# Attention over a convolution block: which PSUM banks hold the turned maxima, the sums and the fourth projection tile, and when the reciprocals run

## What is computed

```
K, Q, V = conv1x1(X, Wq, bq), conv1x1(X, Wk, bk), conv1x1(X, Wv, bv)   # 8 heads of 64
M   = einsum('bhmn,bhen->bhme', K, V)          # 64 x 64 per head
Out = conv1x1(einsum('bhme,bhmn->bhen', M, Q), Wo, bo) + X
x1  = batch_norm(Out)                          # over batch and points

xn      = group_norm(x1)                       # 32 groups
q, k, v = split(w_qkv @ xn + b_qkv)            # 8 heads of 64
weight  = softmax(q.T @ k / sqrt(64))          # 1024 x 1024 per head
out     = x1 + w_proj @ (v @ weight.T) + b_proj
```

## Time and profile before

| | us |
|---|---|
| median of 3 runs | 2682.73 (2681.97 to 2682.75) |
| the profiled execution | 2683.36 |
| its span, first to last instruction | 2681.8 |
| PE busy | 2582.5 (96%) |
| DVE busy | 1621.5 (60%) |
| POOL busy | 1164.3 (43%) |
| ACT busy | 964.6 (36%) |
| mean granted clock of PE | 0.99 of full |

### The profile page before, as it was taken

One profiled execution on the slowest core, in us unless ns is written; L12 is line 12 of the kernel. 1 busy time (PEld: TensorE's weight loads), 2 busy tenths in 40 slices (PEclk: granted clock), 3 DMA queues, 4 the chain that ended last, 5 costly groups with the idle time before them and its releaser, 6 DMA issues.

```text
span 2681.8 us, 38121 instructions
## 1 busy us (share of the span) xinstructions
PE 2582.5 (96%) x13876; PEld 1710.9 (64%) x13876; DVE 1621.5 (60%) x1756; ACT 964.6 (36%) x1154; POOL 1164.3 (43%) x590
## 2 busy tenths in 40 slices
PE   7999999997999999999999999999999999999998
PEld 6888888886655665565557555755665565557554
DVE  6555455545576737755764667467647746664665
ACT  3333223332343433433442443343433433432433
POOL 4230000000276546564573676375654645761762
PEclk9999999999999999999999999999999999999999
DMA  5330111113202230231205111401231141103001
GB/s 185 130 132 33 47 47 63 63 63 111 110 24 79 87 126 24 95 128 70 102 17 181 40 79 61 152 24 80 102 110 41 78 175 38 79 18 109 17 16 63
DMA packets 64195, 214.34 MB, mean 80 GB/s; under 512 B 9152, under 2 KB 9152, under 8 KB 63168
## 3 DMA queue, kind: packets, MB, share of 16 engines
q1 hardware_dynamic: 49504, 159.41, 16.5%
q0 software_dynamic: 14560, 52.96, 5.4%
HBM read 141.05 MB, written 71.30 MB: 79 GB/s over the span
## 4 chain that ended last, share of the span: by engine, by line
PE 72%; DVE 15%; issue 6%; POOL 4%; ACT 2%; DVEq 0%; ACTq 0%; POOLq 0%
PE psum L1135 16%; PE psum L1380 14%; PE psum L1363 11%; PE psum L1320 7%; PE psum L1154 6%; PE psum L1330 5%; DVE a_all L999 4%; POOL a_all L528 4%; PE psum L1178 4%; PE psum L1206 3%; DVE small L964 3%; DVE r_all L955 2%; DVE r_all L1032 2%; ACT r_all L632 1%; PE psum L1252 1%
## 5 line engine op out<-in xcount | busy, mean ns | idle before, releaser
L528 POOL TENSOR_TENSOR a_all<-a_all 128x1024 f32<-128x1024 f32 x410 | 989.9, 2414 | 715.5 <-ACT a_all L701 680.6
L964 DVE TENSOR_REDUCE small<-psum 128x2 f32<-128x1024 f32 x481 | 589.3, 1225 | 377.8 <-PE psum L1330 377.6
L701 ACT ACTIVATE a_all<-psum 128x1024 f32<-128x1024 f32 x512 | 496.4, 1021 | 496.7 <-PE psum L1363 491.7
L1363 PE MATMUL psum<-r_all 64*128 64x512 f32 x4096 | 517.6, 391 | 1.5 <-ACT a_all L701 1.4
L1380 PE MATMUL psum<-a_all 128*64 128x512 f32 x2048 | 495.7, 605 | 1.4 <-DVE a_all L999 1.4
L1135 PE MATMUL psum<-r_all 128*128 128x512 f32 x1920 | 452.3, 393 | 7.0 <-DVE r_all L1032 5.8
L1363 PEld LDWEIGHTS psum<-r_all 64*128 64x128 f32 x4096 | 385.2, 185 | 88.9 <-ACT a_all L701 11.0
L1135 PEld LDWEIGHTS psum<-r_all 128*128 128x128 f32 x1920 | 357.6, 188 | 101.8 <-DVE r_all L837 11.6
L1320 PE MATMUL psum<-r_all 128*128 128x512 f32 x1536 | 377.2, 402 | 30.6 <-issue 11.8
L1320 PEld LDWEIGHTS psum<-r_all 128*128 128x128 f32 x1536 | 290.5, 192 | 133.6 <-DVE r_all L955 32.7
L1380 PEld LDWEIGHTS psum<-a_all 128*64 128x64 f32 x2048 | 124.3, 136 | 230.4 <-issue 174.0
(11 more groups left out here) (130 smaller groups left out, 1866.0 us busy)
## 6 DMA issues: line engine op xcount, KB each, us to landing
r_all<-w_dram SPq DMA_DIRECT2D x48, 1024.0 KB, 4.9
xn_dram<-a_all POOLq DMA_DIRECT2D x56, 512.0 KB, 3.8
r_all<-xn_dram SPq DMA_DIRECT2D x7, 4096.0 KB, 15.3
a_all<-y_dram SPq DMA_DIRECT2D x9, 2048.0 KB, 7.8
a_all<-x SPq DMA_DIRECT2D x16, 1024.0 KB, 6.6
y_dram<-a_all SPq DMA_DIRECT2D x16, 1024.0 KB, 4.2
out<-a_all SPq DMA_DIRECT2D x32, 512.0 KB, 3.2
w_dram<-r_all POOLq DMA_DIRECT2D x16, 512.0 KB, 3.6
```

Source lines behind the costliest of these rows:

```text
L528: pool.tensor_tensor(p_sum[:, :, cols], probs[:, 0, :, cols] if i == 1 else p_sum[:, :, cols], probs[:, i % SLOTS, :, cols], ALU.add).then ...
L701: act.activation(probs[:, i % SLOTS, :, cols], psum[half][:, :, :], ACT.Exp, scale=SCALE).then_inc(probs_ready, 1)
L964: dve.reduce_max(max2[:, :, tile, half], psum[3][:, :, :], AX_X).then_inc(work_free, 2)
L1363: last = pe.matmul(psum[half][:, h], k[rows_], q[rows_], start=(t == 0), stop=(t == 3))
```

## The change

1. The turned maxima go to psum[0] (`turn_full`, `turn_read`) instead of a bank of the ring. The scores' first half waits for `turn_read`. At p = 0 the turn now comes ahead of the first projection tile.
2. The sums go to psum[1]. ACT copies them to `recip` in SBUF (`copy_sums`, after the first HI part), and the scores' second half waits for that copy. DVE inverts them in place in eight pieces of 128 columns: two after each of max_rows, LO 1 and LO 2, one after maximum tiles 1 and 3.
3. The fourth projection tile goes to psum[2] (`fourth_full`, `fourth_free`), the bank of the weighing. All 16 maximum tiles go to psum[3]; `max_first` goes away.
4. DVE makes the LO part of the fourth tile after maximum tile 0, normalise after tiles 5 and 7, hid_lo after 9 and 11. ACT makes the HI part of the normalised values after score tiles 3 and 4. The two copies of `next_norm` move from p = 1 to p = 0, ahead of the maxima.
5. After p = 3 the pieces stand behind v tiles 1 to 4, normalise behind 5, hid_lo behind 6 and 7.
6. The batch loops of the second part on ACT, DVE and PE are made with `hint_back_edge=True`.
7. The matmuls for M take 128 columns of w_q (`part`) instead of 256 (`window`).

```diff
@@ ACT
+            def copy_sums(pairs):
+                act.wait_ge(o_normed, ONE + pairs * NH)
+                act.wait_ge(sums_full, ONE + pairs + 1)
+                act.activation(recip, psum[1][:, :, :], ACT.Copy).then_inc(sums_copied, 1)
...
                     for i in range(QK):
-                        if more and p and i == QK - 1:
-                            hid_hi(b, p - 1, 0)
                         if more:
-                            qk_hi((p + 1) % PAIRS, par, i)
-                        if i == 0:
-                            work.next()
+                            qk_hi((p + 1) % PAIRS, par, i, pairs + 1 if i == QK - 1 else None)
+                        if p and i == 0:
+                            copy_sums(pairs - 1)
...
-                        if p and more and i == 0:
-                            hid_hi(b, p - 1, 1)
+                        if p and more and i in (3, 4):
+                            hid_hi(b, p - 1, i - 3)
...
-            with act.Fori(0, B - 2) as b:
+            with nc.Fori(0, B - 2, engines=[act.engine], hint_back_edge=True) as b:
@@ DVE
-                        of = bank(g)[part, g % 2 * P + e * D:g % 2 * P + e * D + D]
+                        of = bank(g)[part, part]
...
-            def invert_sums(pairs, h):
-                if h == 0:
-                    dve.wait_ge(sums_full, ONE + pairs + 1)
-                    dve.wait_ge(o_normed, ONE + pairs * NH)
-                dve.reciprocal(recip[:, h], psum[2][:, h]).then_inc(sums_read, 1)
+            def invert_sums(pairs, first, n):
+                if first == 0:
+                    dve.wait_ge(sums_copied, ONE + pairs + 1)
+                for piece in range(first, first + n):
+                    part = recip[:, piece // CT, piece % CT * P:(piece % CT + 1) * P]
+                    dve.reciprocal(part, part).then_inc(sums_inverted, 1)
...
-                    next_qk(0)
+                    if p:
+                        next_qk(0)
                     max_rows(pairs)
-                    if p:
-                        invert_sums(pairs - 1, 0)
+                    if not p:
+                        next_qk(0)
+                    if p and more:
+                        invert_sums(pairs - 1, 0, 2)
                     next_qk(1)
-                    if p:
-                        invert_sums(pairs - 1, 1)
+                    if p and more:
+                        invert_sums(pairs - 1, 2, 2)
                     next_qk(2)
-                    if p:
-                        normalise(pairs - 1, 0)
-                    next_qk(3)
+                    if p and more:
+                        invert_sums(pairs - 1, 4, 2)
...
-                        max_first(pairs)
-                        if p:
-                            normalise(pairs - 1, 1)
-                        for m in range(1, MAXES):
+                        for m in range(MAXES):
                             max_tile(m)
-                            if p and m <= NH:
-                                hid_lo(b, p - 1, m - 1)
+                            if m == 0:
+                                next_qk(QK - 1)
+                            if p:
+                                if m in (1, 3):
+                                    invert_sums(pairs - 1, 6 + m // 2, 1)
+                                if m in (5, 7):
+                                    normalise(pairs - 1, m // 7)
+                                if m in (9, 11):
+                                    hid_lo(b, p - 1, m // 11)
...
-                        normalise(pairs - 1, 1)
+                        invert_sums(pairs - 1, 0, PIECES)
+                        for h in range(NH):
+                            normalise(pairs - 1, h)
...
-            with dve.Fori(0, B - 2) as b:
+            with nc.Fori(0, B - 2, engines=[dve.engine], hint_back_edge=True) as b:
@@ PE
-                        window = slice(g // 2 * 2 * P, (g // 2 + 1) * 2 * P)
+                        part = slice(g * P, (g + 1) * P)
...
-                            pe.matmul(bank(g)[:, 0:2 * P], ts[:, t, o, g * P:(g + 1) * P], w_q[:, w, o, window],
+                            pe.matmul(bank(g)[:, 0:P], ts[:, t, o, part], w_q[:, w, o, part],
...
-                            pe.matmul(bank(g)[:, 0:2 * P], u3[:, g * P:(g + 1) * P], bq3[:, window],
+                            pe.matmul(bank(g)[:, 0:P], u3[:, part], bq3[:, part],
...
-                piece, cols, to = i // 2, slice(i % 2 * HALF, (i % 2 + 1) * HALF), next_tile()
+                piece, cols = i // 2, slice(i % 2 * HALF, (i % 2 + 1) * HALF)
+                to = psum[2][:, 0] if fourth else next_tile()
...
-                pe.transpose(next_tile()[:, 0:P], max_cols.rearrange("p h t -> p (h t)"), eye).then_inc(work_full, 1)
-                return work.upto()
+                pe.transpose(psum[0][:, 0, 0:P], max_cols.rearrange("p h t -> p (h t)"), eye).then_inc(turn_full, 1)
...
+                    if i == 0 and half == 0:
+                        pe.wait_ge(turn_read, pairs + 1)
+                    if i == 0 and half == 1:
+                        pe.wait_ge(sums_copied, ONE + pairs)
...
-                        pe.wait_ge(sums_read, ONE + pairs * NH)
                         if more:
-                            pe.wait_ge(max0_read, pairs + 1)
+                            pe.wait_ge(fourth_free, pairs + 1)
...
-                pe.wait_ge(o_ready, ONE + pairs + 1)
+                pe.wait_ge(probs_ready, ONE + (pairs + 1) * 2 * NT)
...
-                        last = pe.matmul(psum[2][h * D:(h + 1) * D, half], ones64, p_sum[:, h, half * HALF:(half + 1) * HALF],
+                        last = pe.matmul(psum[1][h * D:(h + 1) * D, half], ones64, p_sum[:, h, half * HALF:(half + 1) * HALF],
...
-                    next_qk(0)
-                    turned = max_turn(pairs)
+                    if p:
+                        next_qk(0)
+                    max_turn(pairs)
                     if p:
                         sums(pairs - 1)
+                    else:
+                        next_qk(0)
                     for i in range(1, QK):
                         next_qk(i)
-
-                    pe.wait_ge(work_free, turned)
                     next_max()
...
-            with pe.Fori(0, B - 1) as b:
+            with nc.Fori(0, B - 1, engines=[pe.engine], hint_back_edge=True) as b:
```

More of the change, by code:

```diff
@@ L625, in norm_row, with qk_hi @@
                 act.activation(hi_slot[:, j % 2], raw[j], ACT.Copy).then_inc(xn_hi_done, 1)
-            def qk_hi(pair, par, i):
-                n, ps = work.next()
-                act.wait_ge(work_full, n)
+            def qk_hi(pair, par, i, fourth=None):
+                if fourth is not None:
+                    ps = psum[2][:, 0]
+                    act.wait_ge(fourth_full, fourth)
+                else:
+                    n, ps = work.next()
+                    act.wait_ge(work_full, n)
                 of_k, cols = i // 2, slice(i % 2 * HALF, (i % 2 + 1) * HALF)
@@ L707, in batch1 @@
                     if more:
-                        for _ in range(MAXES - 1):
+                        for _ in range(MAXES):
                             work.next_pair()
@@ L723, in batch1 @@
                     norm_rows(range(1))
+                if not last:
+                    copy_sums(b * PAIRS + PAIRS - 1)
                 for h in range(NH):
@@ L947, in _, with qk_lo @@
             work = Tally()
-            def qk_lo(pair, par, i, count):
-                n, ps = work.next()
+            def qk_lo(pair, par, i, count, fourth=False):
+                ps = psum[2][:, 0] if fourth else work.next()[1]
                 of_k, cols = i // 2, slice(i % 2 * HALF, (i % 2 + 1) * HALF)
@@ L1111, in batch1 @@
                         v_tile(b + 1, i)
-                        if i in (1, 2):
-                            invert_sums(pairs, i - 1)
-                        if i in (3, 4):
-                            normalise(pairs, i - 3)
-                        if i in (5, 6):
-                            hid_lo(b, PAIRS - 1, i - 5)
+                        if 1 <= i <= 4:
+                            invert_sums(pairs, 2 * (i - 1), 2)
+                        if i == 5:
+                            for h in range(NH):
+                                normalise(pairs, h)
+                        if i in (6, 7):
+                            hid_lo(b, PAIRS - 1, i - 6)
                 for t, (o, half) in enumerate(proj_tiles(last)):
@@ L1332, in max_tile @@
                 last.then_inc(work_full, 2)
-            def max_first(par, pairs):
-                pe.wait_ge(sums_read, ONE + pairs * NH)
-                for h in range(2):
-                    rows_ = slice(h * D, (h + 1) * D)
-                    last = pe.matmul(psum[2][:, h], q_hl[rows_, par, HI, 0:P], k_hl[rows_, par, HI, 0:HALF], start=True, stop=True)
-                last.then_inc(max0_full, 1)
             def max_turn(pairs):
```

(3 more changed lines are left out.)

75 lines of the change are left out of this document (37 added, 38 removed).

## The result

The changed kernel takes 2690.57 us (median of 9 runs, 2689.13 to 2692.38) against 2682.73 of 9 runs of the kernel before: a ratio of 1.0028, with a 95% interval of 1.0018 to 1.0039. It is slower by 8 us, or 0.3%, where the forecast was 2735.5, about 53 us slower.

The account below looks back on a forecast made before the run. TensorE (PE), busy 2582.5 of 2681.8 us, was taken as the bound. 2683.4 - 19.4 - 11.6 - 30.8 - 2.5 + 74.8 + 41.6 = 2735.5 us, range 2662 to 2748.

Parts of the forecast that it names:

- Narrower M products: 416 block-diagonal matmuls at 128 columns: 0.22 us each, at plain fp32's passes, instead of 0.120; +41.6 us.
- rival (2): Narrow matmuls keep the transposes' pace, -6 for +41.6, the rest holds: 2687.9 us, near no change; chance 0.28.
- back edges: Batch loop's back edges: the hint removes six PE issue gaps and the clock loss behind them; -19.4 us.
- the turn at p = 0: First pair of eight batches: turned maxima in psum[0] spare the next projection tile its 1.45 us wait; -11.6 us.
- last pair and tail: First weighing no longer waits for reciprocals, nor the last sums for ACT's copy; -2.5 us.
- Maxima and scores at p > 0: Pairs after the first: DVE's side work no longer delays the maxima, 1.29 us a pair; with two copies moved, -30.8 us.
- the side work beside POOL: Normalise and hid_lo moved beside POOL's additions at p > 0 cost 3.4 us in each of 22 pairs; +74.8 us.
- the lockstep of 5.2 us: DVE side operations and POOL's additions lock in step: two maximum tiles take 5.2 us instead of 4.36, 0.85 lost.
- the first loss of 0.9: The first DVE side operation beside POOL meets any phase, 0 to 1.4 us; taken as 0.9.
- The reciprocal piece at tile 3: The eighth piece, read from SBUF, also waits beside POOL: 0.5 us a pair, an upper end of +11 us.
- the gains of 64.3: All predicted gains together, 64.3 us, set against the narrow matmuls' 41.6 if side operations beside POOL are cheap.

Follow-up runs that it names:

- e1: The changed kernel with the 256-column window of the M products restored: 2692.19 us, ratio to the kernel before 1.0035.
- e9: The kernel before with the 416 M products at 128 columns, nothing else changed: 2682.39 us, ratio 0.9998.
- e10: The kernel before with the back-edge hints on the loops of ACT, DVE and PE, nothing else changed: 2665.54 us, ratio 0.9938.
- e4: The changed kernel with the hints on the three batch loops taken away: 2706.33 us, ratio to the kernel before 1.0090.
- e5: The changed kernel with normalise after maximum tiles 8 and 9, hid_lo after 10 and 11: 2640.77 us, ratio to the kernel before 0.9854.
- e7: The changed kernel with reciprocal pieces 3, 3, 2 among the projection tiles, normalise after maximum tiles 0 and 1, hid_lo after 2 and 3: 2629.96 us.
- e8: The changed kernel with reciprocal pieces 3, 3, 2, normalise after maximum tiles 0 and 1, hid_lo after 8 and 9: 2619.21 us, ratio to before 0.9764.
- e6: The changed kernel with both normalise after maximum tile 8 and both hid_lo after tile 13: 2787.66 us, ratio to the kernel before 1.0398.

## Why the prediction was wrong

**The step that failed** is "Narrower M products": +41.6 in the sum, at most 4 us of gain in the trace (416 x (0.111 - 0.120) = -3.7), and nothing in the time (e1, e9). I took the price of plain fp32, four passes a column, as the nearest in kind. The nearest row in form, the 128-column transposes at 0.106 us, was the right one; the forecast had it as an end and gave it to rival (2). What failed is a mis-sized term, and with it the size of the whole: without it the sum is 2693.9, with -3.7 it is 2690.2, and 2690.6 was measured.

Rival (2), at 0.28, was what happened: 2687.9 for the whole. The Trainium skill (TensorE: Matmul & The Clock Gate, "Back-to-back issue gap") gives about 81 ns per matmul of 128 columns. This kernel's trace does not agree for fp32r: 111 ns.

That the rest comes within 0.4 us is luck. The starts of the turned maxima in the two traces (L1344 before, L1361 after; after, less the 2.86 us of the tile that now stands behind it) split the 9.1 us by which the span grew:

| part | forecast, us | measured, us |
|---|---|---|
| back edges | -19.4 | -21.2 |
| the turn at p = 0, eight pairs | -11.6 | -14.4 |
| maxima, scores and side work at p > 0, 22 pairs | -30.8 + 74.8 = +44.0 | +48.7 |
| last pair and tail, from p = 2 of the last batch | -2.5 | -4.3 |
| all ahead of the second part, M products among it | +41.6 | +0.3 |

(Back edges and side work at p = 3 lie in one stretch; e10's trace, which has the hints alone, parts them. It is one trace of each kernel; e1's reaches the second part 1.1 us later than the changed kernel's.) Each row but the last is off by 2 to 5 us, and these errors cancel. In the last row the M products gain 0.4 us in each of the last six batches (48 of them take 5.56 us from first to last start, not 5.96) and lose it to the slower clock of the first, which no term had.

**Point by point.**
- Back edges, -19.4: right. 15.8 us by undoing it (e4), 18.1 by doing it alone (e10), where 3.8 us were lost elsewhere. PE's issue gaps and the clock behind them went; whether ACT and DVE needed the hint was not tried.
- The turn at p = 0, -11.6: right in kind. The stretch from the start of a pair p = 0 to the next pair was 48.24 us in the seventh batch before, where no lower clock disturbs it (2208.88 to the first projection tile of the next), and is 46.66 us after in the second batch (turn at 967.34, next turn at 1016.86 less the 2.86 of the tile ahead of it): 1.6 us; in the first six batches it is 1.9. No run undoes this move alone.
- Maxima and scores at p > 0 (-30.8) and the side work beside POOL (+74.8): 52.3 us for a pair was forecast, 52.47 measured; the lockstep of 5.2 us shows as 5.23, the first loss of 0.9 as a wait of 1.09. e5, e7 and e8 moved the same operations and won 49.8, 60.6 and 71.4 us, where the waiting rule had let me expect 49, 46 and 75. e6 was expected to win 68 and lost 97: there too the operations end 0.55 us after an addition, but the second of two in a row waited for the next addition, which the expectation had not seen, and the clock fell behind it. So this step, and with it most of the slowdown, is shown. The -30.8 was not isolated by a run of its own; the pairs of e8, at 48.9 to 49.2 us, come down to the 48.87 that it rests on.
- The reciprocal piece at tile 3, an upper end of 11 us: it does not wait (0.94 us beside POOL).
- Last pair and tail, -2.5: from the last sums to the end of the span there are 70.6 us after (2620.28 to 2690.9) and 74.1 before (2607.70 to 2681.8), 3.5 less. Most of that, nearly 3 us, is clock: before, the granted clock from 2606.6 to 2613.4 was 0.51, behind a wait for POOL of 3.4 us ahead of these sums that is not there after. The forecast knew the wait, but gave neither its going nor that clock a price.
- POOL's additions do not get late in the changed kernel: PE waits for them 0.9 us in all. In e8, with shorter pairs, they do.

The direction was right, and so was most of the reason: the gains are real, and the side work beside POOL takes them back. e8, with the side work moved out of the way, is 64 us faster than the kernel before, as the gains of 64.3 in the forecast say. But slower by 0.3% is what the forecast's own rival (2) called near no change, on either side; the part of the direction that rested on the +41.6 was wrong.

## What to carry to other kernels

When a small operation is moved on an engine that shares something with another, ask what the other is doing at that point, and at what phase: here four operations of 0.7 us a pair cost 71 us more at one place than at another (the changed kernel against e8). Before a term rests on a row of another kind, look for the row of the same form, and if the two are 48 us apart, the forecast has two likeliest cases. A hint on the back edges of a long loop was worth 18 us here (e10), for three edited lines.

## What the hardware showed that I had not expected

- fp32r matmuls that each load 128 x 128 weights stand 0.120, 0.112, 0.111 and 0.110 us apart with 256, 192, 128 and 64 columns: from 192 down a narrower one brings hardly any time.
- Narrower matmuls can cost PE its clock: with 64 columns the grant fell to 0.50 in every batch, in the third behind 5.0 us in which PE was busy throughout; with 128 it was 0.50 from 50.5 to 64 us, in the first batch of the changed kernel (0.62 in e9), where with 256 it was 0.89 (0.87 in e1). What in the narrower matmuls does it was not tested.
- Between two waiting DVE operations, one right behind the other, POOL gets its turn (3.86 us for two of 0.7). Spread over two tiles (e5) they cost less than together (e6).
